# Attention scores for the row maxima as 128-row products over zero-padded keys, with the style product moved

## What is computed

```python
y  = clip((x * style) @ weight.T * dcoefs + bias, -256, 256)       # "style product", per batch
Q, K, V = y @ Wq, y @ Wk, y @ Wv                                   # 16 heads in 4 groups share K and V, 64 wide
raw = einsum('bsgwe,btge->bstgw', Q, K / 8)
A   = einsum('bstgw,btge->bsgwe', softmax(raw, axis=2), V)
x   = x + y + A @ Wpost
kx  = modulated_linear(x, ...)                                     # 16 small heads of 8
out = softmax(kx_h . kx_j / sqrt(8)) mixed over kx                 # inside one token, head against head
x   = x + ffn(modulated_linear(out, ...))                          # top 2 of 8 experts
```

## Time and profile before

| | us |
|---|---|
| median of 3 runs (lowest, highest) | 617.47 (617.37, 618.84) |
| the profiled execution's own time | 620.54 |
| its span, first to last instruction | 618.7 |
| PE busy (share of the span) | 599.2 (97%) |
| PEld | 506.5 (82%) |
| DVE | 461.6 (75%) |
| ACT | 345.2 (56%) |
| POOL | 277.4 (45%) |
| mean granted PE clock | 0.983 of full |

### The profile page before, as it was taken

How to read it: one execution, slowest core, us unless ns; L and a number is a source line. 1 busy time by engine, 2 the same in 40 slices (tenths; PEclk the granted TensorE clock), 3 DMA queues, 4 the chain that set the end, 5 groups by cost and what they waited for, 6 DMA issues and landing times. The chain is left out here.

```text
span 618.7 us, 15704 instructions
## 1 busy us (share of the span) xinstructions
PE 599.2 (97%) x4772; PEld 506.5 (82%) x4772; DVE 461.6 (75%) x1089; ACT 345.2 (56%) x759; POOL 277.4 (45%) x248
## 2 busy tenths in 40 slices
PE   8899999999999999999999999999999897899998
PEld 8788888888888888888888888888888796566765
DVE  4235777788887888878888787887787799677676
ACT  2656666666666666666666666666665421534443
POOL 1002656565656565555555555656565573000000
PEclk9999999999999999999999999999999986799999
DMA  7300000000000000000000000000000000000004
GB/s 239 75 2 2 1 4 1 0 0 0 0 0 0 0 0 0 0 0 0 0 0 0 0 0 0 0 0 0 0 0 1 2 1 0 2 0 0 0 0 136
DMA packets 9363, 7.18 MB, mean 12 GB/s; under 512 B 1088, under 2 KB 8832, under 8 KB 9216
## 3 DMA queue, kind: packets, MB, share of 16 engines
q1 hardware_dynamic: 9344, 6.94, 3.7%
HBM read 4.84 MB, written 2.10 MB: 11 GB/s over the span
## 5 line engine op out<-in xcount | busy, mean ns | idle before, releaser
L1061 POOL TENSOR_TENSOR pair<-kx 128x1152 f32<-128x1152 f32 x32 | 82.2, 2568 | 200.7 <-ACT kx L822 197.9
L588 PE MATMUL bank_a<-v,prob 128*128 128x65 f32 x1024 | 131.7, 277 | 3.5 <-ACT prob L822 2.2
L588 PEld LDWEIGHTS bank_a<-v,prob 128*128 128x128 f32 x1024 | 121.7, 191 | 13.4 <-ACT prob L822 10.2
L272 DVE TENSOR_REDUCE row_max<-bank_s 128x4 bf16<-128x512 f32 x128 | 88.9, 695 | 57.1 <-PE bank_s L563 57.0
L1056 POOL TENSOR_TENSOR mix_hi<-mix_hi 128x512 f32<-128x512 f32 (+2 forms) x96 | 107.4, 1119 | 7.5
L822 ACT ACTIVATE prob<-bank_t 128x512 f32<-128x512 f32 x128 | 69.5, 594 | 16.5 <-PE bank_t L578 15.6
L822 ACT ACTIVATE attT<-misc 128x512 f32<-128x512 f32 x64 | 38.1, 595 | 71.2 <-PE misc L602 71.2
L595 PE MATMUL misc<-yT,wq_sb 128*128 128x128 f32 x512 | 73.9, 288 | 0.4 <-DVE yT L423 0.4
L595 PEld LDWEIGHTS misc<-yT,wq_sb 128*128 128x128 f32 x512 | 61.9, 191 | 7.1 <-DVE yT L423 0.6
L578 PE MATMUL bank_t<-qT,kT 64*128 64x256 f32 x512 | 65.7, 376 | 0.0
L1049 POOL TENSOR_TENSOR mix_hi<-weight,kx 128x1024 f32<-128x1024 f32 x32 | 62.8, 1964 | 4.4 <-ACT weight L822 4.4
(11 more groups left out here) (149 smaller groups left out, 995.7 us busy)
## 6 DMA issues: line engine op xcount, KB each, us to landing
out<-acc_all SPq DMA_DIRECT2D x8, 256.0 KB, 2.3
x_all<-in_xT SPq DMA_DIRECT2D x1, 1024.0 KB, 9.7
w_sb<-in_w SPq DMA_DIRECT2D x2, 512.0 KB
x_all<-in_xT SPq DMA_DIRECT2D x1, 768.0 KB, 7.5
wq_sb<-in_wq SPq DMA_DIRECT2D x1, 512.0 KB, 6.2
wpost_sb<-in_wpost SPq DMA_DIRECT2D x1, 512.0 KB, 9.8
x_all<-in_xT SPq DMA_DIRECT2D x1, 256.0 KB, 3.7
b_rows<-in_b SPq DMA_DIRECT2D x16, 4.0 KB
```

The lines of the kernel that those rows point to most:

```text
L272: V.tensor_reduce(bass.AP(row_max, max_row(g), [[HPG * P, P], [P + 1, HPG]]).unsqueeze(2), bank_s[:, :, :], AX.X, ALU.max).then_inc(s_max, 1)
L588: last = mm(att_bank(g)[:, w, :], prob[:, g % 2, w, :], v1[:, j, g, :], start=(w == 0), stop=True, skip_group_check=True)
L1061: G.tensor_tensor(pair[:, :, :], bass.AP(kx2, jc * 2 * P, [[4 * P, P], [0, SHIFTS], [1, P]]), bass.AP(kx2, jc * 2 * P, [[4 * P, P], [MD, S ...
```

## The change

Three things change.

1. The bf16 keys `k16` get a slot for each half of the partitions: `k16[rows, ja, pair, half, :]` holds the keys of the group on these partitions, and the other half of the partitions holds zeros from a memset at the start. A score product then takes all 128 partitions of queries (two groups) against 256 columns (both groups' keys, padded), and gives one head of two groups at once. A round is two such products instead of four, still 128 x 512 results in `bank_s`. ACT copies the keys in two instructions of 64 partitions.
2. A round now covers two heads w of a pair of groups, so the maxima are written by `heads_max` with another pattern. The rounds stay four a slot.
3. The style product of the next batch moves: on PE from ahead of `mix`'s transposition to behind the second `scores_t` and the product of L734, on ACT from ahead of `mixT` to behind the fourth exponential, and on DVE the clamp from ahead of the maxima of rounds 0 and 1 to behind them. POOL's order is unchanged.

```diff
-        k16 = sb("k16", [P, 2, PAIRS, P], BF16)
+        k16 = sb("k16", [P, 2, PAIRS, 2, P], BF16)
...
+            V.memset(k16[:, :, :, :, :], 0.0).then_inc(s_zero, 1)
...
-            def group_max(s, g):
-                dve.wait_ge(s_s_mm, 4 * s + g + 1)
+            def heads_max(s, i):
+
+                p, first_w = i // 2, i % 2 * 2
+                dve.wait_ge(s_s_mm, 4 * s + i + 1)
                 need(dve, s_neg_mm, n(s - 1))
-                V.tensor_reduce(bass.AP(row_max, max_row(g), [[HPG * P, P], [P + 1, HPG]]).unsqueeze(2),
-                                bank_s[:, :, :], AX.X, ALU.max).then_inc(s_max, 1)
+                V.tensor_reduce(bass.AP(row_max, first_w * (P + 1) + HPG * p, [[HPG * P, P], [P + 1, 2], [KEY, 2], [1, 1]]),
+                                bank_s[:, :, :].rearrange("p (w h) t -> p w h t", h=2), AX.X, ALU.max).then_inc(s_max, 1)
...
+                if A:
+                    heads_max(a, 0)
+                    heads_max(a, 1)
                 if has(a + 1):
                     dve.wait_ge(s_y_raw, n(a + 1))
                     need(dve, s_kv_mm, n(a))
                     need(dve, s_xy, n(a))
                     V.tensor_scalar(yT[:, :], misc[0][:, 1, :], CLAMP, -CLAMP, ALU.min, ALU.max).then_inc(s_yT, 1)
-                if A:
-                    group_max(a, 0)
-                    group_max(a, 1)
...
-                rows = slice(KEY * (g % 2), KEY * (g % 2 + 1))
-                for w in range(HPG):
-                    last = mm(bank_s[:, w, :], q16[rows, j, g // 2, w, :], k16[rows, j, g // 2, :],
+                for w in range(2):
+                    last = mm(bank_s[:, 2 * w:2 * w + 2, :], q16[:, j, g // 2, g % 2 * 2 + w, :], k16[:, j, g // 2, :, :],
                               start=(w == 0), stop=True, skip_group_check=True)
...
-                    f(k16[:, ja, :, :], misc[0][:, 0:2, :]).then_inc(s_k16, 1)
+                    for half in range(2):
+                        rows = slice(KEY * half, KEY * (half + 1))
+                        f(k16[rows, ja, :, half, :], misc[0][rows, 0:2, :]).then_inc(s_k16, 1)
```

More of the change, by code:

```diff
@@ L225, in col @@
             return bass.ds(b * P, P)
-        def max_row(g):
-            return KEY * (g % 2) + HPG * (g // 2)
         block = ctx.enter_context(nc.Block())
@@ L265, in _ @@
             V.tensor_tensor(demod[:, :, :], newton[:, :, :], inv_root[:, :, :], ALU.mult).then_inc(s_demod, 1)
-            dve.wait_ge(s_zero, 4)
+            dve.wait_ge(s_zero, 5)
             dve.wait_ge(s_owned, 3)
-            def group_max(s, g):
-                dve.wait_ge(s_s_mm, 4 * s + g + 1)
+            def heads_max(s, i):
+                p, first_w = i // 2, i % 2 * 2
+                dve.wait_ge(s_s_mm, 4 * s + i + 1)
                 need(dve, s_neg_mm, n(s - 1))
-                V.tensor_reduce(bass.AP(row_max, max_row(g), [[HPG * P, P], [P + 1, HPG]]).unsqueeze(2),
-                                bank_s[:, :, :], AX.X, ALU.max).then_inc(s_max, 1)
+                V.tensor_reduce(bass.AP(row_max, first_w * (P + 1) + HPG * p, [[HPG * P, P], [P + 1, 2], [KEY, 2], [1, 1]]),
+                                bank_s[:, :, :].rearrange("p (w h) t -> p w h t", h=2), AX.X, ALU.max).then_inc(s_max, 1)
             def invert(s, g):
@@ L339, in slot @@
                 if B:
-                    group_max(s, 3)
+                    heads_max(s, 3)
                 if D:
@@ L432, in slot @@
                 if A:
-                    group_max(a, 2)
+                    heads_max(a, 2)
             slots(dve, slot)
@@ L551, in _ @@
             pe.wait_ge(s_owned, 3)
-            pe.wait_ge(s_zero, 4)
+            pe.wait_ge(s_zero, 5)
             pe.wait_ge(s_ld_qkv, 48)
@@ L702, in slot @@
                     nc.tensor.transpose(misc[1][:, 0, :], kxT[:, :], ident[:, :]).then_inc(s_kxn_mm, 1)
[L703 to L708, removed]
                 if D:
@@ L725, in slot @@
                 if A:
-                    pe.wait_ge(s_k16, n(a))
+                    pe.wait_ge(s_k16, 2 * n(a))
                     scores(a, ja, 0)
@@ L734, in slot @@
                     mm(misc[2][:, 0, :], modw_sb[:, 2, :], mixT[:, :], start=True, stop=True).then_inc(s_o_mm, 1)
+                if has(a + 1):
+                    if A:
+                        pe.wait_ge(s_v, n(a))
+                        pe.wait_ge(s_k16, 2 * n(a))
+                    pe.wait_ge(s_xs, n(a + 1))
+                    mm(misc[0][:, 0, :], modw_sb[:, 0, :], xs[:, j, :], start=True, stop=True).then_inc(s_y_mm, 1)
                 if B:
@@ L836, in _ @@
             act.wait_ge(s_demod, 5)
-            act.wait_ge(s_zero, 4)
+            act.wait_ge(s_zero, 5)
             def exp_scores(s, g):
@@ L937, in slot @@
                       misc[1][:, 0:1, :].to_broadcast([P, 2, P])).then_inc(s_kx2, 1)
[L938 to L943, removed]
                 if D:
@@ L955, in slot @@
                     exp_scores(s, 3)
+                if has(a + 1):
+                    act.wait_ge(s_y_mm, n(a + 1))
+                    need(act, s_yT, n(a))
+                    act.wait_ge(s_demod, 5)
+                    f(misc[0][:, 1, :], misc[0][:, 0, :], ACT.Identity, scale=demod[:, 0, bass.ds(a + 1, 1)],
+                      bias=modb_sb[:, 0:1]).then_inc(s_y_raw, 1)
                 if D:
```

## The result

| | before | after |
|---|---|---|
| median (lowest, highest), us | 617.63 (617.37, 618.84) | 657.44 (655.30, 658.61) |
| the profiled execution's own time | 620.54 | 658.61 |
| its span | 618.7 | 656.8 |
| PE busy | 599.2 (97%) | 606.1 (92%) |
| DVE busy | 461.6 (75%) | 508.9 (77%) |

The account below looks back on a forecast made before the run. PE was taken as the bound, at 14.77 us a slot. 28 x (16.35 - 14.77) = +44.2, -2.6 and -0.3 give +41 on 620.5; the median 3 lower is 658.8, four low-clock slots make 655; range 630 to 675.

Parts of the forecast that it names:

- What bounds the kernel: In the loop, PE sets the pace, busy 395.5 of 397 us at full clock; a slot takes 14.77 us.
- 0.30 us for a 64-row round between full-height work: On PE, changing between 128 and 64 array rows costs 0.30 us a round; three rounds a slot save 0.90.
- PE's floor: The slot length that PE alone would need after the change: 13.7 us.
- The third rival: On PE, zero-padded full-height products still cost 0.3 around; slots stay 14.6 to 14.8, 612 to 618 us; chance 0.03.
- The clamp as the new zero: New slot laid out from the clamp `yT` on DVE, now behind the second maximum; POOL's `xs` starts at 0.37 us.
- The turns: POOL and DVE take whole instructions in turn on two SBUF tensors; the first halving add costs 1.15 us more.
- `pair` 0.25 to 0.3 ahead of `shifted`: POOL's `pair`, before 0.38 us behind DVE's `shifted`, now starts first and holds it throughout; chance 0.78.
- It comes again in every slot: The collision of `pair` and `shifted` repeats in every full slot, at 16.35 us a slot.
- four slots of low clock as relief: Four slots starting at 1.2 GHz keep `shifted` in the lead and take about 15.4 us, -0.95 each.
- ACT's second key copy at nothing: On ACT, the second key copy of 0.3 to 0.4 us stands where ACT waits, so no step waits for it.
- The filled wait of 0.2: On PE, the moved style product, 0.22 us, fills the wait of 0.2 us ahead of the third `attend`.

Follow-up runs that it names:

- e3: Changed kernel with POOL's head mixing (`mix_hi` and its adds) ahead of its wait for the clamp: 592.2 us, ratio 0.955 to before.
- e8: The kernel of e3 but with the old 64-row rounds, so the moved style product and POOL's head mixing first: 613.49 us.
- e10: The kernel of e1 with ACT copying the values ahead of the bf16 keys: 596.73 us, ratio 0.962 to before.
- e5: Changed kernel with `pair` issued on POOL as two instructions, of five and four shifts: 632.82 us, ratio 1.020 to before.
- e2: The move of style product, scaling and clamp alone, with the old 64-row rounds: 613.92, 627.17, 631.57 and 647.96 us in four executions.
- e4: Changed kernel with `pair` on POOL also waiting until `shifted` of the same slot is done: 598.74 us, ratio 0.966 to before.
- e9: Changed kernel with ten unread dummy products on PE ahead of the third `attend`, where PE waits: 664.48 us, ratio 1.073 to before.
- e1: Changed kernel with style product, scaling copy and clamp in their old places, so the padded keys alone: 604.6 us, ratio 0.975 to before.
- e7: The kernel of e1 with POOL's head mixing ahead of its wait for the clamp: 604.94 us, ratio 0.973 to before.
- e11: The kernel of e2 with `pair` waiting for `shifted`: 611.1 to 618.8 us in six executions, ratio 0.992 to before.
- e6: Changed kernel with twenty unread dummy products on PE ahead of the third `attend`: 712.09 us.

## Why the prediction was right, and where its sizes were off

- **What bounds the kernel: right.** With PE's work cut and its waits left out (e3) the time falls by 28 us, nearly all of it PE's slot (14.77 - 13.93 = 0.84, 31 times 26).
- **0.30 us for a 64-row round between full-height work: the steps were right, the saving was put too high.** Four transpositions last 0.44 until the round starts (385.91 - 385.47), and the round 0.22 (386.13 - 385.91), where the earlier trace rows had 0.54 and 0.32. The Trainium skill ("TensorEngine Tiling (Array Packing)", Key Properties) says that a change of tiling mode drains TensorE, and the trace agrees; it gives no price. e8 to e3 gives 0.62 a slot, not 1.0, and PE's floor, taken as 13.7, came out as 13.93. The missing part is short waits that were hidden before. L732 starts 0.3 ahead of the third `attend` in the spared slots of the changed kernel and in e3 alike, where two products take 0.22. More lies around the last round. PE in e3:

```profile
242.60 1.07 PE L593 MATMUL misc<-yT,wq_sb 128*128 128x128 f32 x8
243.51 0.63 PE L600 MATMUL misc<-ident,att 128*128 128x128 f32 x4
244.16 0.39 PE L561 MATMUL bank_s<-k,q 128*128 128x256 bf16 x2
244.39 1.14 PE L593 MATMUL misc<-yT,wq_sb 128*128 128x128 f32 x8
```

Four transpositions last 0.65 until this round starts, and 0.52 in every other slot, instead of 0.44. At 244.03 DVE ends the third maximum, which frees `bank_s`; it now stands behind the clamp as well. Eight queries behind a round last 0.91 to 0.98 instead of the 0.89 that e10 shows where nothing holds them. Together this is some 0.35 a slot, and the prediction had 0.1 of it. The third rival, no saving at all, is out.
- **The clamp as the new zero, and POOL hung on it: right**, by the table. This is the step that a list of added and removed instructions doesn't hold.
- **The turns: right as a mechanism.** The Trainium skill ("SBUF — State Buffer", SBUF: two separate sides) calls the pair of ports that DVE and GpSimd share an exclusive lock, held by whoever starts first for the whole instruction; e5 and e2 show just that. At the first halving add the order was the one laid out: `mix_lo` started 0.09 us ahead of it and took 1.22, and the turn fell on L349 (1.65).
- **`pair` 0.25 to 0.3 ahead of `shifted`: right**, 0.26 measured, and by e4 it is the whole loss. The margin was as thin as said: a `pair` later by 0.3 us would have turned the sign, as e4 shows by force. For the other slot of a loop turn it was thinner still, which the prediction did not see, as it read one slot only. The two kinds of slot differ already in the kernel before:

```profile
238.23 0.42 DVE L398 TENSOR_TENSOR shifted<-score,h_max 128x256 f32<-128x256 f32 x1
```

```profile
238.80 2.57 POOL L1061 TENSOR_TENSOR pair<-kx 128x1152 f32<-128x1152 f32 x1 [6.03 <-ACT kx L822]
```

Here `shifted` leads by 0.57, not by 0.38 as in the slot that was read. At full clock (e9) `pair` gets ahead in this kind by 0.02 to 0.04 us only. In the changed kernel these are the slots that are spared.
- **"It comes again in every slot": wrong.** 14 slots collide, where the prediction had 24 of 28 (all but four). The term that was mis-sized is the clock. I took four slots of low clock as relief, -0.95 each. The trace has a low-clock stretch behind every collision, which lengthens the colliding slot or its successor (17.1 and 16.3 for 16.35) and spares the successor its own collision (16.2 and 15.3 for 15.4). The mean of all is 16.2, and 28 x (16.2 - 14.77) = +40; the forecast had 44.2 - 3.8 = +40.4 for the same 28 slots. Two errors, too many collisions and too little lost to the clock, nearly cancel. By the prediction's own prices, 14 spared slots would have made 658.8 - 13.3 = 645.5; what the clock costs beyond them, 0.3 us in the mean of the colliding slots and 0.3 in that of the spared ones, gives 9 us back. So that the forecast of 655 lies so near to 657.4 is luck; the sign and the mechanism are not. e9 bounds the relief from the other side: without the low clock it is 664.
- **ACT's second key copy at nothing: right here, for a reason that I did not give.** In e1 and e10 the key copies cost 8 us with the style product in its old place, where it waits for the copy of the values behind them. The cover is the move itself.
- **The filled wait of 0.2**: the move gives 12.7 us once the collision is away (e7 to e3), more than 0.2 a slot, since the cost of the key copies goes with it. From e10, which doesn't have that cost, to e3 it is 4.5 us, 0.16 a slot.

What stays open: the rest of e11's spread, and why a low-clock stretch is now 3.4 and now 6.9 us long.

## What to carry to other kernels

When an instruction is moved, ask who is released by it and lay out the new slot from there: here a change that cut PE's work by 0.6 us a slot lost 6%, because POOL was released by a clamp that now came later, and met DVE on SBUF. A lead of a few tenths of a microsecond between a short DVE instruction on the critical path and a long POOL one is worth a wait or a reordering: one wait turned 657 into 599, and putting POOL's independent work ahead of its wait gave 592. Before believing a sum that comes out right, test its largest terms one by one.

## What the runs showed of the hardware that I had not expected

- Whichever of `pair` and `shifted` starts first goes first, down to 0.01 us. In the traces of e2, e5, e6 and e9 `pair` went first in every meeting in which its row starts 0.01 us or more ahead, and `shifted` in every other. In e2 the two starts fall together, and it took 614 to 648 us in four executions.
- Waits of 2.26 us on PE are followed by stretches of 3.4 or 6.9 us at 1.2 GHz (in e2 up to 10.2), though PE is busy throughout them, and such a stretch can be of use: it moved work apart that collides at full clock (e9, 1% slower at clock 1.00).
